# The experts' running sums and the residual added on VectorE instead of GpSimd, in a fused conditioned-FFN kernel

## What is computed

```python
def _more_forward(x, Wg, bg, W1, b1, W2, b2):
    cur = x
    for r in range(R):                     # R = 4 rounds
        flat = cur.reshape(-1, h)
        logits = flat @ Wg[r] + bg[r]
        vals, idx = jax.lax.top_k(logits, TOPK)          # 2 of E = 4
        w = jax.nn.softmax(vals, axis=-1)
        cw = jnp.sum(jax.nn.one_hot(idx, E) * w[..., None], axis=1)
        hmid = jax.nn.gelu(jnp.einsum('nh,ehf->enf', flat, W1) + b1[:, None, :])
        y = jnp.einsum('enf,efh->enh', hmid, W2) + b2[:, None, :]
        out = jnp.einsum('ne,enh->nh', cw, y)
        cur = cur + out.reshape(b, s, h)
    return cur
# x = x + _more_forward(conditioned(x)); x = x + gated_ffn(conditioned(x))
```

## Time and profile before

| | us |
|---|---|
| median of 3 runs | 485.16 |
| lowest, highest | 484.31, 489.13 |
| the profiled execution | 486.61 |
| span of its profile | 484.8 |

### The profile page before, as it was taken

One profiled execution on the slowest core, in us unless ns is written; L12 is line 12 of the kernel. 1 busy time (PEld: TensorE's weight loads), 2 busy tenths in 40 slices (PEclk: granted clock), 3 DMA queues, 4 the chain that ended last, 5 costly groups with the idle time before them and its releaser, 6 DMA issues.

```text
span 484.8 us, 7478 instructions
## 1 busy us (share of the span) xinstructions
PE 477.9 (99%) x2270; PEld 397.0 (82%) x2270; DVE 387.7 (80%) x641; ACT 393.9 (81%) x542; POOL 118.7 (24%) x102
## 2 busy tenths in 40 slices
PE   7999999999999999999999999999999999999997
PEld 7998888888888888888888888888888887888885
DVE  4789899999879898988898898889897758554343
ACT  3799988888888888988888888888888888697653
POOL 5796212121212112121222121231313144400000
PEclk9999999999999999999999999999999999999999
DMA  7702702020201102020202012120202000000001
GB/s 209 215 5 88 266 18 89 2 87 3 87 11 76 71 16 87 0 87 0 87 0 87 11 76 82 49 89 0 87 2 87 2 0 0 1 0 1 0 22 69
DMA packets 6986, 26.30 MB, mean 54 GB/s; under 512 B 2226, under 2 KB 2610, under 8 KB 4786
## 3 DMA queue, kind: packets, MB, share of 16 engines
q1 hardware_dynamic: 5826, 21.20, 12.1%
q0 software_dynamic: 528, 3.67, 2.2%
q10 hardware_dynamic: 608, 1.11, 0.8%
HBM read 24.81 MB, written 1.18 MB: 54 GB/s over the span
## 4 chain that ended last, share of the span: by engine, by line
PE 96%; DMA 2%; SPq 1%; issue 0%; DVE 0%
PE bank L505 34%; PE bank L506 34%; PE bank L509 26%; DMA stage<-lora_all 2%; PE bank L594 1%; PE bank L595 1%; PE bank L527 1%; SPq L244 0%; SPq L247 0%; PE bank L540 0%; PE bank L524 0%; SPq L257 0%; DVE x L1276 0%; SPq L345 0%; SPq L344 0%
## 5 line engine op out<-in xcount | busy, mean ns | idle before, releaser
L812 ACT ACTIVATE act_out<-bank,vec 128x512 f32<-128x512 f32 x256 | 165.4, 682 | 41.8 <-PE bank L509 32.6
L1115 DVE TENSOR_TENSOR hid_lo<-act_out,hid_hi 128x1024 fp32r<-128x1024 f32 x128 | 156.6, 1243 | 33.3 <-ACT hid_hi L817 33.2
L817 ACT ACTIVATE hid_hi<-act_out 128x1024 fp32r<-128x1024 f32 x128 | 135.9, 1062 | 8.0 <-PE bank L509 0.2
L468 POOL TENSOR_TENSOR cur<-cur,prod 128x512 f32<-128x512 f32 x48 | 64.9, 1352 | 238.4 <-DVE prod L1126 237.9
L505 PE MATMUL bank<-hid_hi,moe_hi 128*128 128x512 f32 x256 | 99.9, 390 | 0.0
L509 PE MATMUL bank<-hid_hi,moe_lo 128*128 128x512 f32 x256 | 99.7, 390 | 0.0
L505 PE MATMUL bank<-xhi,moe_hi 128*128 128x512 f32 x256 | 99.7, 390 | 0.0
L506 PE MATMUL bank<-hid_lo,moe_hi 128*128 128x512 f32 x256 | 99.7, 389 | 0.0
L506 PE MATMUL bank<-xlo,moe_hi 128*128 128x512 f32 x256 | 99.6, 389 | 0.0
L509 PE MATMUL bank<-xhi,moe_lo 128*128 128x512 f32 x256 | 99.6, 389 | 0.0
L505 PEld LDWEIGHTS bank<-hid_hi,moe_hi 128*128 128x128 f32 x256 | 48.1, 188 | 11.3 <-issue 0.2
(11 more groups left out here) (126 smaller groups left out, 569.9 us busy)
## 6 DMA issues: line engine op xcount, KB each, us to landing
cw_all<-cw_dram SPq DMA_DIRECT2D x16, 1024.0 KB, 4.6
stage<-ffn_w POOLq DMA_DIRECT2D x1, 2304.0 KB, 8.5
cw_all<-moe_w SPq DMA_DIRECT2D x4, 512.0 KB, 10.3
stage<-lora_all SPq DMA_DIRECT2D x5, 160.0 KB, 7.1
x<-x_t POOLq DMA_DIRECT2D x3, 256.0 KB, 7.0
out_t<-x SPq DMA_DIRECT2D x3, 256.0 KB, 2.5
cur<-cond_base ACTq DMA_DIRECT2D x2, 256.0 KB, 3.1
stage<-ffn_w POOLq DMA_DIRECT2D x1, 512.0 KB, 3.8
```

The source lines that it names most:

```text
L468: pool.tensor_tensor(cur[:, c, :], cur[:, c, :], prod[:, s % 2, :], ALU.add).then_inc(add_done, 1)
L812: act.activation(act_out[:, f // 2, f % 2, :], bank[:, f, :], ACT.Gelu_apprx_tanh, bias=vec[:, V_B1 + e * FC + f:V_B1 + e * FC + f + 1]).t ...
L817: act.activation(hid_hi[:, s % 2, 2 * pr:2 * pr + 2, :], act_out[:, pr, :, :], ACT.Copy)\
L1115: dve.tensor_tensor(hid_lo[:, s % 2, 2 * pr:2 * pr + 2, :], act_out[:, pr, :, :], hid_hi[:, s % 2, 2 * pr:2 * pr + 2, :].bitcast(F32), ALU ...
```

## The change

`mixture_add` on GpSimd goes. VectorE's `mixture_sum` now makes the sum of every expert right behind its product, and in the last round, for e = 0, the residual's add between the two. The product still waits for the sum of two steps before. GpSimd has no instruction in the rounds but the second load of weights, now issued as soon as the first two low pieces are made, and the reduction of the maximum.

```diff
--- before.py
+++ after.py
@@ -454,19 +454,6 @@
             moe_low(3)
             moe_low(7)
 
-            def mixture_add(rnd, s, last):
-
-                n, c, e = STEPS * rnd + s, s // EXPERTS, s % EXPERTS
-                if e == EXPERTS - 1:
-                    return
-                pool.wait_ge(prod_done, n + 1)
-                pool.wait_ge(add_done, ADD0 + n)
-                if last and e == 0:
-
-                    pool.tensor_tensor(cur[:, c, :], cur[:, c, :], x0[:, c, :], ALU.add).then_inc(res_done, 1)
-                    pool.wait_ge(res_done, c + 1)
-                pool.tensor_tensor(cur[:, c, :], cur[:, c, :], prod[:, s % 2, :], ALU.add).then_inc(add_done, 1)
-
             pool.wait_ge(xs_done, CHUNKS)
             for i in range(2):
                 pool.memset(prod[:, i, 0:1], 0.0).then_inc(add_done, 1)
@@ -475,16 +462,10 @@
             pool.wait_ge(first_lo_done, 1)
             pool.wait_ge(cw_ready[0], 16)
             pool.dma_start(ffn_raw, ffn_w[:, 0:RING, :]).then_inc(ffn_in[0], 16)
-            with pool.Fori(0, ROUNDS - 1) as rnd:
-                for s in range(STEPS):
-                    mixture_add(rnd, s, False)
             pool.wait_ge(ffn_lo_done, LATE)
             pool.dma_start(ffn_raw[:, 0:LATE, :], ffn_w[:, RING:FFN_PIECES, :]).then_inc(ffn_in[1], 16)
-            for s in range(STEPS):
-                mixture_add(ROUNDS - 1, s, True)
-                if s == PREP_AT[LATE - 1] + 1:
-                    pool.wait_ge(low_max_done, FFN_PIECES + 1)
-                    pool.partition_all_reduce(low_any[:], low_row[:], P, bass.bass_isa.ReduceOp.max).then_inc(low_any_done, 1)
+            pool.wait_ge(low_max_done, FFN_PIECES + 1)
+            pool.partition_all_reduce(low_any[:], low_row[:], P, bass.bass_isa.ReduceOp.max).then_inc(low_any_done, 1)
             for c in range(CHUNKS):
                 t = hidden_at(GATED, c)
                 pool.wait_ge(hi_done, LO_MOE + 2 * t + 1)
@@ -1116,7 +1097,7 @@
                                       hid_hi[:, s % 2, 2 * pr:2 * pr + 2, :].bitcast(F32), ALU.subtract)\
                        .then_inc(lo_done, 1)
 
-            def mixture_sum(rnd, s):
+            def mixture_sum(rnd, s, last):
 
                 n, c, e = STEPS * rnd + s, s // EXPERTS, s % EXPERTS
                 if e == 0:
@@ -1125,10 +1106,13 @@
                 dve.wait_ge(add_done, n + 1)
                 dve.scalar_tensor_tensor(prod[:, s % 2, :], bank[:, 4 + s % 2, :], vec[:, V_B2 + e:V_B2 + e + 1],
                                          cw_all[:, c % 2, e, :], ALU.add, ALU.mult).then_inc(prod_done, 1)
-                if e == EXPERTS - 1:
-                    dve.wait_ge(prod_done, n + 1)
-                    dve.wait_ge(add_done, ADD0 + n)
-                    dve.tensor_tensor(cur[:, c, :], cur[:, c, :], prod[:, s % 2, :], ALU.add).then_inc(add_done, 1)
+                dve.wait_ge(add_done, ADD0 + n)
+                if last and e == 0:
+
+                    dve.tensor_tensor(cur[:, c, :], cur[:, c, :], x0[:, c, :], ALU.add).then_inc(res_done, 1)
+                    dve.wait_ge(res_done, c + 1)
+                dve.wait_ge(prod_done, n + 1)
+                dve.tensor_tensor(cur[:, c, :], cur[:, c, :], prod[:, s % 2, :], ALU.add).then_inc(add_done, 1)
 
             def round_steps(rnd, last):
                 for s in range(STEPS):
@@ -1144,7 +1128,7 @@
                         project_low(c - 1)
                     if last and s == STEPS - 1:
                         return
-                    mixture_sum(rnd, s)
+                    mixture_sum(rnd, s, last)
                     if e == 1 and not (last and c >= CHUNKS - 2):
                         gate_logits((c + 2) % CHUNKS, rnd + (c + 2) // CHUNKS)
                         gate_order((c + 2) % CHUNKS, rnd + (c + 2) // CHUNKS)
@@ -1289,7 +1273,7 @@
                                                      vec[:, V_S2 + f:V_S2 + f + 1], silu[:, f, :],
                                                      ALU.mult, ALU.mult).then_inc(unit_done, 1)
                             if c == 0 and f == 1:
-                                mixture_sum(ROUNDS - 1, STEPS - 1)
+                                mixture_sum(ROUNDS - 1, STEPS - 1, True)
                             if c == CHUNKS - 1 and f == 1:
                                 stage_low(t - 1, 1)
```

## The result

The median is 496.35 us (494.7 to 497.84, four runs) against 485.55 us of the kernel before on the same chip. The ratio is 1.0227, with a 95% interval of 1.0201 to 1.0253: slower. The profiled execution took 497.09 us (its span 495.0), against 486.6 (484.8) before.

A forecast was written before the change was run, and what follows sets the result against it. TensorE, without gaps, was taken as the bound, made to wait by VectorE's longer queue. Round 0's 2.1, rounds 1 and 2's 3.2 and the last round's 0.9 gave 6.2 us more: 491.3 us, range 487.5 to 498.

The forecast's parts named there:

- What bounds the kernel: TensorE, busy 99% of the span and without gap in a round, so whatever lengthens a round must make it wait.
- What a sum costs: On VectorE's in-order queue, each sum behind its product adds 0.72 us, 2.16 a chunk; bounds 0.61 to 0.81.
- What VectorE had to pay with: VectorE's waits per chunk: 1.6 us with a weight piece, 3.3 in chunk 3, to set against the sums.
- The handshake: ScalarE's hidden tiles keep VectorE's first split of one pair 6.05 us from the next pair's second: 0.39 us a chunk.
- GpSimd's silence: VectorE's splits and weight pieces, no longer held by GpSimd's adds, give back 0.16 us a chunk.
- The sum for a chunk: Excess over the 22.26 us period: 0.8 us in chunks 1 and 2, 0.7 in chunk 0, -0.7 in chunk 3.
- The last round: Residual's add and sums on VectorE there: 0.1 us for chunk 0, 0.8 for chunk 1, nothing after; 0.9 in all.
- The clock: Sign of a wrong forecast: a lower granted clock beside TensorE's gaps, which no earlier row allowed to be priced.
- the dear case: Rival: 33 sums at 0.81 us (3.0 more) and chunk 3's spare time unusable (2.1): 11.3 more, 496.5 us; chance 0.17.
- The absorbed case: Rival: VectorE's slack takes the sums and TensorE hardly waits; 487.9 us if only the handshake wait is missing; chance 0.29.
- The faster case: Rival: a sum on the path at the last chunk's end would win 0.6 us on VectorE: 484.6 us; chance 0.02.

The follow-up runs named there:

- waits_swapped: The changed kernel with the sum's two waits in the other order (product first), except the last round's e=0: 493.32 us, ratio 1.0158.
- filled: The changed kernel with an instruction due anyway (gate work) put between product and sum in e=0, 1 and 2: 486.95 us, ratio 1.0045.
- pool_dummy: The changed kernel, with GpSimd adding zeros into spare memory where it made the sums in rounds 0 to 2, plus one add before: 496.14 us, ratio 1.0225.
- vec_last: The changed kernel with the sums of rounds 0 to 2 given back to GpSimd; VectorE makes sums and residual in the last round: 486.87 us, ratio 1.0034.
- weights_first_last: The changed kernel with the gate's weights, in the last round only, moved between the product of e=0 and the residual's add: 494.16 us, ratio 1.017.
- after_again: The changed kernel run again without an edit: 495.46 us against 485.08, ratio 1.0206.
- short_max: The changed kernel with the row maximum of a weight piece reading 8 of 512 columns, part of the computation left out: 490.79 us, ratio 1.0119.

## Why the prediction was right, and where it was not

The forecast was 491.3 us, slower, with a range of 487.5 to 498; the median is 496.35. Side and range held. The forecast's own band, 490 to 494.5, did not hold it: the rise is 10.8 us where 6.2 was forecast.

- **What bounds the kernel.** Held. Every microsecond lost is a wait of TensorE for VectorE or a lower clock behind one. In the rounds TensorE waits for the splits of H_3, none in chunk 3 (22.26, busy 22.26), as forecast. VectorE is busy for 94 to 95% in chunks 0 and 1 of round 1, just under the 95% named as a sign.
- **What a sum costs.** 0.72 was forecast; the change has 0.85 + 0.61 - 0.67 = 0.79 (166.75, 167.59, 168.20). I had taken the 0.78 of the earlier trace rows for a property of the two instructions. But the order of the two waits had changed, the wait for the product had gone from the sum to a semaphore instruction ahead of it, and `waits_swapped` shows that this is worth 0.07. The 0.09 credited to chunk 0 came to 0.02 (161.83 to 162.68 is 0.85 instead of 0.87).
- **What VectorE had to pay with.** Held in size: one sum a chunk is free, two cost 0.9 us in all, the third is charged almost in full.
- **The handshake.** Held. p0 of H_0 at 164.47 (in the change's round 1) to p1 of H_1 at 170.52 is 6.05 us, the bound that was worked out; the wait is 0.27 instead of 0.39, because the sum ahead of it takes longer. In `filled` it shows as 0.47.
- **GpSimd's silence.** 0.70 for a weight piece was forecast, 0.69 measured; no split takes 1.7. The measured fall of 0.03 us a split and 0.1 a weight piece is at most 0.36 a chunk, where 0.16 was stated, and stands against 2.4 for three sums at 0.79. The Trainium skill, "SBUF — State Buffer" (the section "Who interferes with whom"), says that a VectorE instruction with two SBUF inputs contends with a GpSimd instruction that reads SBUF; the trace of `pool_dummy` agrees (a split of 2.36 us beside GpSimd's add, 1.22 without). The rule is borne out, and the relief is still too small to matter.
- **The sum for a chunk.** Chunks 1 and 2: 0.8 forecast, 1.0 measured; the 0.2 is three sums at 0.07. Chunks 3 and 0 together: nothing forecast, 0.24. Rounds 1 and 2: 1.6 each forecast, 2.3 each measured. Round 0: 2.1 forecast, 2.85 measured (0.52, 1.05, 1.28). All of it 5.3 against 7.4; `waits_swapped`, which has the price that I had reckoned with in ten of a round's sixteen sums, still has 6.2; no run tells what the rest is made of.
- **The last round is the step that failed.** It was costed at 0.9 us: 0.1 for chunk 0 and 0.8 for chunk 1. Chunk 0 measured 0.2. Chunk 1 and what follows measured 3.8: 2.1 of delay ahead of the projection and 1.7 of matmuls at the lower clock. I had followed only the queue from the splits to TensorE. The projection waits for another result of the same queue, the reading of the gate's bank, which stands directly behind the residual's add and the sum; it had 0.79 us in hand before, readable within 0.15 in the trace (342.06, 343.00), against a lag of 2.9. `vec_last` and `weights_first_last` show it.
- **The clock.** Named among the signs of a wrong forecast, and it came, though not beside the gaps of 0.7 to 1.0 us in the rounds, where it stays 1.00.
- **The rivals.** The forecast of the dear case was 496.5, close to the time, but by luck, since it came another way: its 0.81 a sum was nearly right (0.79), its other term was not, since chunk 3's spare time was usable. The absorbed case decides at 0.6 us a sum; `filled`, at 0.57 for the sum shown, comes out at 486.95, near it, though the 487.9 that I gave it was reckoned from a missing handshake wait and not from a cheaper sum. The faster case fell with the waits, as argued.

Of the excess over the forecast the rounds have 2.1 us (7.4 against 5.3) and the last round 3.1 (4.0 against 0.9). That the range still held is owed to its width: the path that brought most of the 3.1 is in none of its terms or rivals.

Not settled: what decides whether the lower clock follows a gap.

## What to carry to other kernels

An idle engine's long instruction can be cheaper than a busy engine's short one: count what a move adds to an in-order queue against the waits that this queue has in each stage, since the first instructions are paid from waits and the next is charged in full. For every instruction behind the inserted one, also look up who else waits for its semaphores (here a bank that is used again) and how many tenths of a microsecond were in hand. If a dependent instruction must stand behind its producer, put one that is due anyway between them: that took 8.5 us of the 10.4 back, 6.2 of them in the rounds. And where an instruction has two waits, look up in the trace which of them it carries itself: the blocking one on an instruction of its own cost 0.07 us each time, 2.1 us of the time in all.

## What was unexpected of the hardware

- The order in which two waits are written ahead of a VectorE instruction changes its start. The wait for the producer ends 0.78 us behind the producer's start in every case; an instruction that carries this wait itself starts then, one behind a separate semaphore instruction at 0.85, one behind a register instruction that carries it at 0.86 to 0.87.
- An independent VectorE instruction behind the 0.74 us product starts 0.66 us later, the dependent one 0.78 to 0.87: the dependence costs 0.1 to 0.2 us each time, though both are on one engine.
- Behind a single gap of 1.96, 1.97 and 1.97 us (the change, `after_again`, `pool_dummy`) on a TensorE busy without pause before it, the granted clock fell in all three profiled executions (0.76, 0.73 and 0.66 in 350:355), while other executions of the same kernels have a mean clock of 1.000; behind single gaps of 1.53, 1.61 and 1.70 us (`vec_last`, `short_max`, `waits_swapped`) it was 1.00 in the profiled executions, and so it was behind all gaps of 0.7 to 1.0 us.
- A GpSimd add that meets a VectorE sum ends 0.89 to 0.90 us behind the sum's end, whether it takes 1.17, 1.44 or 1.53 us; a VectorE split that meets a GpSimd add ends 1.08 and 1.10 behind the add's end. The recorded starts don't tell who is held: the split of 2.36 us is recorded 0.21 ahead of GpSimd's add, and it is the split that pays.
